# Weighting the values in blocks of four steps instead of two, in an attention block with adaptive layer norm

## The reference, cut to what matters

```python
h = _layernorm(x) * (1 + ca) + sa
q = (h @ Wq.T)                      # 8 heads of 64
kv_latent = h @ Wkv_down.T          # 64 columns, shared by the heads
k, v = kv_latent @ Wk_up.T, kv_latent @ Wv_up.T
attn = softmax(einsum('bqhd,bkhd->bhqk', q, k) * 64 ** -0.5)
x = x + ga * (einsum('bhqk,bkhd->bqhd', attn, v) @ Wo.T)
h = _layernorm(x) * (1 + cb) + sb
x = x + gb * (h @ weight.T + pooled(h) @ disha)
```

## Time and profile before

| what | value |
|---|---|
| median of 3 runs | 3203.18 us (3201.83 to 3203.7) |
| the profiled execution, its time | 3202.91 us |
| its span, first to last instruction | 3201.1 us |
| granted TensorE clock, mean | 0.997 of full speed |
| busy: PE, DVE, ACT, POOL | 99%, 69%, 53%, 81% of the span |

### The profile page before, as it was taken

The page is one execution under the profiler, slowest core; times in us unless marked ns, Lnnn a source line. Parts: engine busy times, 40 slices in busy tenths (PEclk is TensorE's granted clock), DMA queues, the critical chain, the costliest instruction groups (busy, mean ns, idle before and its releaser), DMA issues. The chain is left out here.

```text
span 3201.1 us, 45110 instructions
## 1 busy us (share of the span) xinstructions
PE 3155.7 (99%) x15394; PEld 1916.2 (60%) x15394; DVE 2198.4 (69%) x2530; ACT 1708.8 (53%) x3209; POOL 2594.8 (81%) x1521
## 2 busy tenths in 40 slices
PE   7999999999999999999999999999999999999997
PEld 5555656656566665666666566665666666666555
DVE  6567676776767767677776777767677676776664
ACT  3555555554555555555555555555555455555544
POOL 3888788887878878788887888878878787887786
PEclk9999999999999999999999999999999999999999
DMA  2111111211112111111111111111120121211111
GB/s 82 37 41 60 47 57 34 76 35 47 57 47 67 34 57 54 47 57 44 47 54 56 58 34 54 57 47 57 43 71 31 48 67 38 67 37 48 47 50 41
DMA packets 161252, 162.91 MB, mean 51 GB/s; under 512 B 58112, under 2 KB 109440, under 8 KB 161024
## 3 DMA queue, kind: packets, MB, share of 16 engines
q1 hardware_dynamic: 161024, 160.03, 15.3%
HBM read 74.40 MB, written 17.33 MB: 29 GB/s over the span
## 5 line engine op out<-in xcount | busy, mean ns | idle before, releaser
L962 POOL TENSOR_TENSOR prob_sum<-prob_sum,probs 128x1024 f32<-128x1024 f32 x768 | 1882.6, 2451 | 243.9 <-ACT probs L803 189.4
L1108 DVE TENSOR_REDUCE neg_max<-ps_max 128x1 f32<-128x1024 f32 x1024 | 1247.6, 1220 | 753.9 <-PE ps_max L634 748.0
L803 ACT ACTIVATE probs<-ps_score 128x512 f32<-128x512 f32 x2048 | 1113.3, 598 | 969.2 <-PE ps_score L611 958.3
L588 PE MATMUL ps_mix<-probs,values 128*64 128x512 f32 x4096 | 991.6, 605 | 0.0
L609 PE MATMUL ps_score<-query,key_hi 128*128 128x512 f32 x2048 | 873.8, 427 | 1.1 <-ACT probs L803 1.1
L611 PE MATMUL ps_score<-query_m,key_lo 128*128 128x512 f32 x2048 | 805.1, 393 | 0.0
L634 PE MATMUL ps_max<-key_hi,query 128*128 128x512 f32 x2048 | 640.7, 394 | 5.0 <-DVE neg_max L1108 3.5
L609 PEld LDWEIGHTS ps_score<-query,key_hi 128*128 128x128 f32 x2048 | 384.7, 188 | 326.8 <-issue 247.0
L588 PEld LDWEIGHTS ps_mix<-probs,values 128*64 128x64 f32 x4096 | 248.4, 136 | 477.8 <-issue 477.0
L962 POOL TENSOR_TENSOR prob_sum<-probs 128x1024 f32<-128x1024 f32 x128 | 328.5, 2567 | 209.2 <-ACT probs L803 208.9
L634 PEld LDWEIGHTS ps_max<-key_hi,query 128*128 128x128 f32 x2048 | 383.8, 188 | 96.6 <-DVE neg_max L1108 5.6
(11 more groups left out here) (197 smaller groups left out, 2832.8 us busy)
## 6 DMA issues: line engine op xcount, KB each, us to landing
query_m<-query SPq DMA_DIRECT2D x128, 512.0 KB, 3.2
recip<-recip_scratch SPq DMA_DIRECT2D x254, 128.0 KB, 2.9
x_in<-in_L_attn_x_dram SPq DMA_DIRECT2D x32, 512.0 KB, 3.9
x_mid<-in_L_attn_x_dram SPq DMA_DIRECT2D x64, 256.0 KB, 4.5
out_dram<-x_mid SPq DMA_DIRECT2D x64, 256.0 KB, 2.2
denoms<-recip SPq DMA_DIRECT2D x508, 1.0 KB, 1.7
gates<-gates_scratch SPq DMA_DIRECT2D x16, 256.0 KB, 4.1
query_m<-max_row SPq DMA_DIRECT2D x128, 4.0 KB
```

The source lines that it names most:

```text
L588: last = nc.tensor.matmul(ps_mix[j * R:j * R + R, :], values[par][:, k, :], probs[:, s % RING, j * HALF:(j + 1) * HALF], start=(k == 0), s ...
L803: nc.scalar.activation(probs[:, s % RING, half * HALF:(half + 1) * HALF], ps_score[half], ACT.Exp, scale=SCALE).then_inc(exps_done, 1)
L962: nc.gpsimd.tensor_tensor(out=total[:, :], in0=before, in1=probs[:, s % RING, :], op=ALU.add).then_inc(adds_done, 1)
L1108: nc.vector.tensor_reduce(neg_max[:, m:m + 1], ps_max[m % 2][:, :], AX_X, ALU.max, negate=True).then_inc(maxima_done, 1)
```

## The change

What it does:

- MIXED goes from 2 to 4: the value matmuls stand in steps with s % 4 = 1, for four steps at once (sixteen records). The ring of exponentials has 6 tiles, and its position runs on over the slots.
- The two `mixed` buffers of 4x1024 columns become one of 11 blocks of 512 columns, in which the batches lie in alternating order (`mixed_block`, `mixed_chunk`).
- PLAN is written anew. Pieces that ScalarE drains (query, `norm_t`, `latent`) stand in steps with s % 4 = 0, most others in steps with s % 4 = 2; steps with s % 4 = 3 have none. Row maxima and denominators stand behind a block. ScalarE puts the drains of a step with s % 4 = 2 off until after the exponentials of the next step (`late`).
- The eight pieces of the output projection become four of twice the size, drained by one add.
- Copies and splits between tiles in SBUF (`mixed_hi/lo`, `h2_split`, the gated weights' halves, statistics) move to steps with s % 4 = 1. GpSimd's jobs move too: apply to step 2, the feed forward's gate to 3, the second norm to 11, 19, 35 and 51, the output's gate to 27, the next apply to 43. MIX_LAG goes from 5 to 4, and a denominator from step 8i+11 to 8i+9.

The core of the diff:

```diff
-RING = 4
+RING = 6
-SPREAD_LAG, RECIP_LAG, OUT_LAG, BACK_LAG, MIX_LAG = 1, 2, 2, 3, 5
-MIXED = 2
+SPREAD_LAG, RECIP_LAG, OUT_LAG, BACK_LAG, MIX_LAG = 1, 2, 2, 3, 4
+MIXED = 4
-AHEAD_LOAD, AHEAD_STATS, AHEAD_APPLY = 44, (48, 49, 50, 51), 53
-NEXT_LOAD, NEXT_STATS, NEXT_APPLY = 61, (0, 1, 2, 3), 4
+AHEAD_LOAD, AHEAD_STATS, AHEAD_APPLY = 22, (29, 33, 37, 41), 43
+NEXT_LOAD, NEXT_STATS, NEXT_APPLY = 47, (1, 1, 1, 1), 2
-OUT_GATES_LOAD, OUT_GATE, OUT_HI, OUT_LO = 44, 52, 54, (56, 59)
-FFN_GATE, FFN_HI, FFN_LO = (1, 8), (3, 9), (3, 11)
+OUT_GATES_LOAD, OUT_GATE, OUT_HI, OUT_LO = 8, 27, 45, (45, 49)
+FFN_GATE, FFN_HI, FFN_LO = (1, 3), (3, 5), (3, 5)
 PLAN = {
-    "query": (40, 42, 50, 58, STEPS, STEPS + 2, STEPS + 4, STEPS + 6),
-    "norm_t": (8, 10, 16, 18),
-    "latent": (26, 32),
-    "values_t": (54, 60),
-    "mixed_hi": (9, 16, 24, 40),
-    "mixed_lo": (10, 17, 25, 41),
-    "out_proj": (12, 14, 20, 22, 30, 36, 44, 46),
-    "norm2": (16, 25, 38, 49),
-    "norm2_t": (24, 34, 48, 56),
-    "h2_split": (25, 35, 49, 57),
-    "ffn": (28, 38, 52, 62),
+    "query": (32, 36, 40, 44, 48, 52, STEPS, STEPS + 4),
+    "norm_t": (8, 12, 16, 20),
+    "latent": (24, 28),
+    "values_t": (42, 46),
+    "mixed_hi": (9, 13, 17, 25),
+    "mixed_lo": (9, 13, 17, 25),
+    "out_proj": (10, 14, 22, 30),
+    "norm2": (11, 19, 35, 51),
+    "norm2_t": (18, 34, 50, 56),
+    "h2_split": (21, 37, 53, 57),
+    "ffn": (26, 38, 54, 62),
 }
-        "max_row": STEPS - NT + 1 + NT * i,
-        "denominator": NT * (i + 1) + 3,
+        "max_row": STEPS - NT + 5 + NT * i,
+        "denominator": NT * (i + 1) + 1,
-        mixed = [sb(f"mixed{i}", [P, PAIRS, T]) for i in range(2)]
+        mixed = sb("mixed", [P, 2 * PAIRS + 3, HALF])
+        def mixed_block(par, p, half):
+            base, count = (0, PAIRS + 1) if half == 0 else (PAIRS + 1, PAIRS + 2)
+            return mixed[:, base + (count - 1 - p if par else p), :]
...
-                        for q, (mp, wp, p) in enumerate(products):
-                            last = nc.tensor.matmul(side[:, 0:D], mp[:, p, j * P:(j + 1) * P],
-                                                    wp[:, p, :], start=(q == 0), stop=(q == len(products) - 1))
+                        for j in range(CT):
+                            for q, (mp, wp, p) in enumerate(products):
+                                pair = PAIRS - 1 - p if (1 - z.par) else p
+                                last = nc.tensor.matmul(side[:, j * D:(j + 1) * D], mp[:, p, j * P:(j + 1) * P],
+                                                        wp[:, pair, :], start=(q == 0), stop=(q == len(products) - 1))
...
-                    if s % NT == 2 and (z.has_o if s < NT else z.has_c):
+                    if s % NT == 1 and (z.has_o if s < NT else z.has_c):
                         g, zg = (s // NT - 1, z) if s >= NT else (GROUPS - 1, flagged(z.o))
                         p, half = divmod(g, 2)
                         need(act, group_done, GROUPS * zg.c + g + 1)
+                        if zg.has_o and p > half:
+                            need(act, mixed_split, CHUNKS * zg.o + 2 * (half + 1))
...
-                    for kind, i, b, w in z.at(s):
+                    late = z.has_c and s % MIXED == 2
+                    for kind, i, b, w in z.at(s - 1) * (z.has_c and s % MIXED == 3) + z.at(s) * (not late):
...
-                        if z.has_o:
-                            full(pool, z, "out_proj", NT - 1)
-                        else:
+                        if not z.has_o:
...
-                            nc.vector.tensor_tensor(x_mid[g][:, j, :], side[:, 0:D], x_mid[g][:, j, :], ALU.add).then_inc(side_drained[room], 1)
+                            nc.vector.tensor_tensor(x_mid[i][:, :, :], side.rearrange("p (j d) -> p j d", j=CT),
+                                                    x_mid[i][:, :, :], ALU.add).then_inc(side_drained[room], 1)
```

More of the change, by code:

```diff
@@ L104 @@
     "mixed_lo": (1, 2, 5, 6),
-    "out_proj": (2, 3, 4, 4, 8, 8, 10, 10),
+    "out_proj": (2, 4, 8, 10),
     "norm2": (4, 5, 9, 11),
@@ L116 @@
     "latent": (6, 8),
-    "query": (10, 12, 50, 58) + PLAN["query"][4:],
+    "query": (10, 12, 50, 52, 57, 58) + PLAN["query"][6:],
     "wo_t": (49, 51),
@@ L307, in adaln_block @@
         w_ffn_gated = x_norm2[:, :, :]
-        stage = [m[:, :, :].rearrange("p a t -> p (a t)") for m in mixed]
+        stage = [probs[:, 2:, :].rearrange("p a t -> p (a t)"), mixed[:, :, :].rearrange("p a t -> p (a t)")]
         s_wmod = stage[0][:, 0:3072].rearrange("p (k n) -> p k n", k=NF)
@@ L816, in slot @@
                         need(act, out_gated, z.c + 1)
+                        if z.has_o:
+                            full(act, z, "out_proj", CHUNKS - 1)
                         nc.scalar.activation(w_out_hi[:, :, :], w_out_gated[:, :, :], ACT.Copy).then_inc(w_out_hi_done, 1)
@@ L830, in slot @@
                             if old >= 0:
-                                for j in range(CT):
-                                    full(act, z, "out_proj", CT * old + j)
+                                full(act, z, "out_proj", old)
                             else:
                                 last_full(act, z)
-                            nc.scalar.activation(mixed_parts(z, g)[0], mixed[1 - z.par][:, :, g * CT * P:(g + 1) * CT * P],
+                            nc.scalar.activation(mixed_parts(z, g)[0], mixed_chunk(1 - z.par, g),
                                                  ACT.Copy).then_inc(mixed_hi_done, 1)
-                    for kind, i, b, w in z.at(s):
+                    if s % NT == 1 and (z.has_o if s < NT else z.has_c):
+                        g, zg = (s // NT - 1, z) if s >= NT else (GROUPS - 1, flagged(z.o))
+                        p, half = divmod(g, 2)
+                        need(act, group_done, GROUPS * zg.c + g + 1)
+                        if zg.has_o and p > half:
+                            need(act, mixed_split, CHUNKS * zg.o + 2 * (half + 1))
+                        nc.scalar.activation(mixed_block(zg.par, p, half), ps_mix[:, :],
+                                             ACT.Copy).then_inc(group_evacuated, 1)
+                    late = z.has_c and s % MIXED == 2
+                    for kind, i, b, w in z.at(s - 1) * (z.has_c and s % MIXED == 3) + z.at(s) * (not late):
                         room, count = z.place(kind, i)
@@ L960, in add_probs @@
                     need(pool, adds_done, done)
-                before = probs[:, (s - 1) % RING, :] if k == 1 else total[:, :]
-                nc.gpsimd.tensor_tensor(out=total[:, :], in0=before, in1=probs[:, s % RING, :], op=ALU.add).then_inc(adds_done, 1)
+                now = STEPS * z.c + s
+                before = probs[:, (now - 1) % RING, :] if k == 1 else total[:, :]
+                nc.gpsimd.tensor_tensor(out=total[:, :], in0=before, in1=probs[:, now % RING, :], op=ALU.add).then_inc(adds_done, 1)
             def slot(z):
@@ L1074, in divide @@
                         p, half = divmod(i, 2)
-                        raw = mixed[mpar][:, p, half * HALF:(half + 1) * HALF]
+                        raw = mixed_block(mpar, p, half)
                         nc.vector.tensor_tensor(raw, raw, recip[:, :], ALU.mult).then_inc(group_mixed, 1)
@@ L1134, in slot @@
                                                     ALU.subtract).then_inc(h_split, 1)
-                    if z.has_n and not first(z) and s in NEXT_STATS:
-                        statistics(z.n, 1, NEXT_STATS.index(s))
+                    for i, t in enumerate(NEXT_STATS):
+                        if z.has_n and not first(z) and s == t:
+                            statistics(z.n, 1, i)
                     for i, t in enumerate(AHEAD_STATS):
```

40 lines of the change are left out of this document (20 added, 20 removed).

## The result

The changed kernel takes 3431.9 us (median of 4 runs, 3427.96 to 3436.96) against 3203.44 (4 runs) of the kernel before: a ratio of 1.0715, interval 1.0696 to 1.0733. The forecast was 3270, range 3160 to 3365. The direction was right, and the time is 162 us above the forecast and 67 above the range. The profiled execution took 3430.65 us (span 3428.8), at a mean granted clock of 0.973, where it was 0.997.

What follows compares the result with a forecast made beforehand. TensorE's queue was taken to set the time: 3202.9 less 61 for longer blocks plus 8 for paired projections gives 3150 us. New waits of 8.5 us in each of 14 slots add 120: 3270 us, range 3160 to 3365.

Steps and rivals of the forecast that it cites:

- steps 24, 38 and 54: Maxima and feed forward pieces wait for VectorE's slowed copies: 1.1 us each, half the upper bounds, 3.4 in a slot.
- What the longer blocks give: TensorE's steps: longer blocks save 61 us, paired output projection pieces lose 8, so 3150 us without new waits.
- Step 9: First denominators wait for GpSimd's adds, queued behind apply and gate: 1.1 to 3.7 us late, taken as 2.4.
- Step 14: Second output projection waits for VectorE's `mixed_lo` behind the multiplication: 0.9 to 4.5 us late, taken as 2.7.
- Every copy meets an add: Rival: VectorE's copies always meet GpSimd's adds, all upper bounds hold, 15.0 us a slot, 3360 us; chance 0.13.
- The shorter queue wins: Rival: TensorE's waits stay near their lower bounds, 3178 us, or 3150 with none; chance 0.30.
- it comes out even: Rival: saving and waits cancel at 3203 us, which takes 3.8 us of waits in a slot; chance 0.07.

Runs made afterwards that it cites:

- experiment 10: Changed kernel with MIX_LAG 5 and most of GpSimd's adds cut to their first 512 columns: 3153.82 us.
- experiment 1: Changed kernel with only MIX_LAG back from 4 to 5, so the multiplication by the reciprocals stands one step later: 3185.14 us, ratio 0.9936 to the kernel before.
- experiment 3: Changed kernel with unread matmuls put into TensorE's waits at steps 14, 38 and 54: 3364.02 us, ratio 1.0496 to the kernel before.
- experiment 11: Changed kernel with MIX_LAG 5 and GpSimd's feed forward gate at step 60 of the slot before instead of step 3: 3175.24 us.

## Why the prediction was right in direction and short in size

The places of the waits and their mechanism were right but for one place. Two steps of the sum failed: the waits at steps 24, 38 and 54 were taken at half of their upper bounds, and the lower clock behind the waits was put at nothing.

*What the longer blocks give: right.* 61 less 8 us, or 3150 without new waits, against 3153.82 in experiment 10; sixteen records take 3.65 us, bare steps there 1.47 to 1.56, and they don't wait for ScalarE in the new order.

*Step 9, 2.4 us: the place was wrong, the mechanism not.* The changed kernel doesn't wait there. The multiplication of step 5 and `w_ffn_lo` behind it hold up VectorE's maxima, so TensorE stands 0.81 us at step 8 first, and by step 9 the adds are ready. Once the multiplication is moved (experiment 1), the wait for GpSimd comes to light, 0.95 us, a little under its lower bound of 1.1.

*Step 14, 2.7 us: the chain was right, one term too small.* Counted from the first score of step 10 (1543.81), the reciprocal was put at 7.9 and came at 7.6, the multiplication at 13.2 and came at 12.8, TensorE at 14.2, where it is in experiment 1, in which nothing holds it up. But I set the multiplication at its median of before, 0.68, and it took 2.02. `mixed_lo` ended at 18.1, the wait is 4.1 us in the mean: near the upper bound of 4.5.

*Steps 24, 38 and 54, 1.1 us each: here the first of the two steps failed.* "I take half" had no row behind it. In step 53 (first score of step 50 at 1680.50) VectorE, GpSimd and TensorE show:

```profile
1690.72 2.28 DVE L1097 TENSOR_TENSOR mixed<-mixed,recip 128x512 f32<-128x512 f32 x1
1692.93 2.84 DVE L1166 TENSOR_TENSOR h_lo<-h_t,h_hi 128x512 fp32r<-128x512 f32 x1
...
1687.58 10.42 POOL L983 TENSOR_TENSOR prob_sum<-prob_sum,probs 128x1024 f32<-128x1024 f32 x4
...
1695.82 0.39 PE L732 MATMUL ps_side<-w_ffn_hi,h_hi 128*128 128x256 f32 x1 [2.38 <-DVE h_lo L1166]
```

The multiplication came at 10.2 (10.0 forecast), the two together took 5.05 (5.1 at their longest), and TensorE would be there at 12.8 as forecast (12.8 in experiment 1). With the clock held up (experiment 3) the three waits are 2.6, 2.7 and 2.7 us: the upper bounds of 2.2 and 2.3 and a little more. Neither of the two finds a gap between adds, since the norm job two steps earlier leaves GpSimd a queue of four adds. So 8.0 us in a slot came from a term put at 3.4.

*The clock behind the waits: the second step that failed; it is not in the sum at all.* 68 us by experiment 3. A wait of TensorE was priced at its own length; it cost a third more (68 us on the 210 between experiments 3 and 10).

So the 162 us that are missing come apart like this. The waits of a usual slot are 12.9 us (0.8, 4.1, 2.6, 2.7, 2.7) instead of 8.5: 14 times 4.4, or 62 us: 1.6 less at steps 8 and 9 together than forecast, 1.4 more at step 14, 4.6 more at the three others. The clock is 68. The other 32 are the rest: the gain's 4, and 22 in the first and last slot, which I had left at no wait (180 and 191 us with the clock held up in experiment 3, the last to the first score of its last step, against 174 and 176 in experiment 10), with a little at the start and end.

*The rivals.* "Every copy meets an add" is what happened at steps 14, 24, 38 and 54: 3360 us was its price, and 3364 is the time with the clock held up. That these agree so well is luck: it had 15.0 us of waits in a slot, 12.9 came, and the first and last slot made up for most of it. I gave it 0.13, on GpSimd's idle shares over the whole span; but copies and adds meet in the block steps, where the queue is full. The Trainium skill, page SBUF — State Buffer, section "Who interferes with whom", spoke for it: it calls the ports that VectorE and GpSimd share an exclusive lock, and lets a VectorE instruction with two SBUF inputs contend with a GpSimd one that reads SBUF. The traces agree: the longest multiplication and the longest copies stand 2.15 to 2.23 us above the shortest of their kind, a little under one add (2.34 at its shortest), and the multiplication's median is back at 0.69 when the adds are halved. "The shorter queue wins" fell with them, though its time, 3178, lies between those of experiments 1 and 11. So did "it comes out even": the waits were 12.9 us in a slot, not 3.8.

## What to carry to other kernels

An instruction that waits for a transfer, or runs long beside another engine's work, is put behind what others need from the same queue; a lag of one step decided between 7% slower and 0.6% faster. When copies on VectorE share a step with a queue of adds on GpSimd, price each of them at its long time, not at its median elsewhere or at half. Price a wait of TensorE with the slower matmuls behind it, and when a wait is removed, look for the next one in the queue that had been hidden by it.

## What the runs showed of the hardware

Behind a wait of 2.4 us in an otherwise busy stretch the granted clock was 0.57 over the next 4 us, and 12 matmuls of 256 columns took 2.26 us (1695.82 to the next score at 1698.08) instead of the 1.40 to 1.42 of experiment 1. In the 14 usual slots these 12 took 1.51 to 2.73 us, so the same wait doesn't always cost the same. Unread matmuls in the wait kept the clock at 1.00.

VectorE pays for its meetings with GpSimd nearly alone here: the multiplication went from 743 to 1825 ns in the mean, while an add of GpSimd took 2481 ns against 2451 before. It can go the other way: where VectorE's copy started first, it took its shortest time and the add behind it was long (the kernel before; such an add takes 2396 ns at its median).

```profile
1447.63 0.68 DVE L1133 TENSOR_TENSOR h_lo<-h_whole,h_hi 128x512 fp32r<-128x512 f32 x1
...
1447.66 2.91 POOL L962 TENSOR_TENSOR prob_sum<-probs 128x1024 f32<-128x1024 f32 x1
```
